# A two-layer transformer block in one launch: the keys of the second attention are split into two parts by GpSimd where they are made, and the first attention's lead-in and the middle stage's end are reordered

## The reference, cut to what matters

```
f1: 16 heads of 8, causal softmax(q k' / sqrt(8) - |i - j|) v, output projection
f2: each token goes to one of 8 experts (argmax): 128 -> 512 -> relu -> 128
f3: 16 heads of 64:
    q, k = rmsnorm(x Wq), rmsnorm(x Wk);  v = x Wv
    scores = q k' / 8 - (i - j) * slope_h * softplus(k . u_h / 8),  causal softmax, times v, projection
f4: 128 -> 512 gated, two 512 x 512 layers with gelu, -> 128
```

## Time and profile before

| | us |
|---|---|
| median of 3 runs | 2282.85 (2277.38 to 2283.62) |
| the profiled execution, its own time | 2285.02 |
| its span, first to last instruction | 2283.2 |
| PE busy | 2072.3 (91%) |
| DVE busy | 1513.8 (66%) |
| ACT busy | 1210.0 (53%) |
| POOL busy | 779.2 (34%) |

### The profile page before, as it was taken

The page is one execution under the profiler, slowest core; times in us unless marked ns, Lnnn a source line. Parts: engine busy times, 40 slices in busy tenths (PEclk is TensorE's granted clock), DMA queues, the critical chain, the costliest instruction groups (busy, mean ns, idle before and its releaser), DMA issues.

```text
span 2283.2 us, 34398 instructions
## 1 busy us (share of the span) xinstructions
PE 2072.3 (91%) x11728; PEld 1169.3 (51%) x11728; DVE 1513.8 (66%) x3409; ACT 1210.0 (53%) x1923; POOL 779.2 (34%) x480
## 2 busy tenths in 40 slices
PE   5899999998487999877999999999999999999998
PEld 2333333334476555544555555555555555655644
DVE  3877777774732778865888878888887875333311
ACT  2366666667343678853656555555565553223232
POOL 5000000000601111003777777777777773000000
PEclk7899999999588999986999999999999999999999
DMA  5233333111265579656666666666666667543300
GB/s 177 95 125 128 120 120 127 57 51 62 98 186 145 172 231 293 200 169 141 170 166 170 165 152 152 150 159 169 163 169 152 164 158 209 135 103 84 88 5 9
DMA packets 230189, 319.11 MB, mean 140 GB/s; under 512 B 22316, under 2 KB 152668, under 8 KB 229608
## 3 DMA queue, kind: packets, MB, share of 16 engines
q1 hardware_dynamic: 214712, 289.04, 46.2%
q0 software_dynamic: 7664, 24.39, 3.0%
q10 hardware_dynamic: 7640, 3.48, 0.5%
HBM read 176.91 MB, written 105.84 MB: 124 GB/s over the span
## 4 chain that ended last, share of the span: by engine, by line
PE 28%; DVE 16%; issue 8%; SPq 1%; DMA 1%; ACT 0%; DVEq 0%
PE ps L1252 10%; DVE a1mx L968 4%; PE ps L916 4%; DVE a1KB L982 3%; DVE a1mx L972 3%; PE ps L900 3%; DVE a1QB L982 3%; PE ps L870 2%; PE ps L901 2%; PE ps L1203 2%; DVE a1mx L965 2%; PE ps L1263 1%; PE ps L1240 1%; PE ps L1241 1%; DVE ps L965 1%
## 5 line engine op out<-in xcount | busy, mean ns | idle before, releaser
L1088 POOL TENSOR_TENSOR a1sum<-a1sum,a1prob 128x1024 f32<-128x1024 f32 (+3 forms) x256 | 489.0, 1910 | 64.9 <-ACT a1prob L1025 33.5
L1025 ACT ACTIVATE a1prob<-ps 128x512 f32<-128x512 f32 (+2 forms) x640 | 326.0, 562 | 252.7 <-PE ps L903 238.4
L468 DVE TENSOR_REDUCE a0grid<-ps 128x8 f32<-128x1024 f32 x288 | 346.7, 1221 | 118.9 <-PE ps L344 64.9
L569 ACT ACTIVATE a0prob<-ps 128x1024 f32<-128x1024 f32 x288 | 292.9, 1025 | 170.2 <-PE ps L370 91.3
L965 DVE CUSTOM_DVE_ANT_0 ps<-ps,c_mask_ij 128x128 f32<-128x128 f32 x496 | 262.7, 551 | 97.2 <-issue 95.5
L900 PE MATMUL ps<-a1QA,a1KA 69*128 69x512 f32 (+3 forms) x768 | 285.7, 379 | 5.8 <-PEq L33 3.4
L916 PE MATMUL ps<-a1prob,a1V 128*64 128x512 f32 (+3 forms) x1536 | 277.9, 505 | 0.0
L870 PE MATMUL ps<-a1KA,a1QA 68*128 68x128 f32 x744 | 241.7, 391 | 28.7 <-DVE a1mx L968 16.4
L901 PE MATMUL ps<-a1QB,a1KB 128*128 128x512 f32 (+3 forms) x768 | 264.4, 352 | 0.0
L916 PEld LDWEIGHTS ps<-a1prob,a1V 128*64 128x64 f32 x1536 | 104.4, 140 | 171.1 <-issue 144.2
L1085 POOL TENSOR_TENSOR a1sum<-a1prob 128x768 f32<-128x768 f32 x64 | 156.8, 2450 | 82.0 <-ACT a1prob L1025 79.9
(11 more groups left out here) (268 smaller groups left out, 3227.5 us busy)
## 6 DMA issues: line engine op xcount, KB each, us to landing
a1FK<-s_k SPq DMA_DIRECT2D x128, 256.0 KB, 5.3
a1FQ<-s_q SPq DMA_DIRECT2D x128, 256.0 KB, 5.8
s_xs<-c_zero POOLq DMA_DIRECT2D x19, 1024.0 KB, 9.0
s_q<-mqkT SPq DMA_DIRECT2D x32, 512.0 KB, 3.0
s_k<-mqkT SPq DMA_DIRECT2D x32, 512.0 KB, 3.0
s_v<-mv SPq DMA_DIRECT2D x32, 512.0 KB, 3.9
a1V<-s_v SPq DMA_DIRECT2D x32, 512.0 KB, 4.4
a1KA<-a1KB SPq DMA_DIRECT2D x64, 256.0 KB
```

The costliest lines, as they stand in the source:

```text
L468: dve.tensor_reduce(grid[g % 2][:, :, a:b + 1:b - a], banks(("max", k)), axis=AX.X, op=ALU.max).then_inc(s1_free, 1)
L569: act.activation(prob[:, :, a:b + 1:b - a, :], banks(("exp", q)), ACT.Exp).then_inc(p_full, 1)
L1025: act.activation(weights_of(g, u)[:, group[0]:group[-1] + 1, off:BANK], both(e, u, group), ACT.Exp).then_inc(weighed, 1)
L1088: pool.tensor_tensor(t[:, :, off:BANK], t[:, :, off:BANK], weights_of(g, u)[:, :, off:BANK], ALU.add).then_inc(summed, 1)
```

## The change

Four things are changed, and buffers are moved to make room for them.

1. **Keys split where they are made.** In the middle, POOL reads each turned tile of k (`qkT`), copies it to a rounded high part KH and subtracts to a low part KL (128 x 1024 each). SP stores both parts, so `k1` in DRAM has two planes; a tile's pair of stores is issued one tile later. The second attention loads high and low straight into KA and KB, so ACT's `split`, DVE's `lower` and the copies of keys go, in the loop and for pair 0 in the middle. For q all is as before, two calls of each in place of four.
2. **The places of what is left.** DVE's two `lower` calls stand at units 0 and 4, ahead of the jobs there; ACT's `split` at units 0 and 3, and the loads in SP's order around them. The q of pair 1 is rounded at the end of the middle.
3. **The first attention's lead-in.** EARLY is 13, there are three high and low buffers, the wait for stored chunks is taken out of `part`, ACT issues the load of BK after product 7 and not 15, and SP issues K and BQ of group 0 after the stores of chunk 2.
4. **The middle's end.** Half of the 24 maxima blocks stand before the last gates and half behind them.

```diff
-    EARLY, NPROD, COL = 17, len(products), dim + 1
+    PARTS3, EARLY, NPROD, COL = 3, 13, len(products), dim + 1
...
-        high, low = ([over(f"{n}{r}", [P, 2, CHUNK], F32R) for r in range(2)] for n in ("high", "low"))
+        high, low = ([over(f"{n}{r}", [P, 2, CHUNK], F32R) for r in range(PARTS3)] for n in ("high", "low"))
...
+            batch_stored(sp, 0)
             still(sp, Q[0], "q0", 0, loaded1[0])
-            sp.wait_ge(cleared, 1)
-            load_second(sp, 0)
             for c in range(2, chunks):
                 store(c)
-                if c == 3:
+                if c == 2:
+                    sp.wait_ge(cleared, 1)
+                    load_second(sp, 0)
+                if c == 4:
                     sp.wait_ge(cleared, 2)
                     load_first(sp, 1)
...
-            for n in range(6, EARLY - 1):
+            for n in range(6, 8):
                 drain(n)
             act.wait_ge(cleared_first, 1)
+            batch_stored(act, 0)
             moving(act, BK[0], "k0", 0, loaded1[0])
-            for n in range(EARLY - 1, NPROD):
+            for n in range(8, NPROD):
                 drain(n)
...
+        def load_a(x, h):
+            if x >= NB:
+                nc.sync.wait_ge(valued, unit(x - NB, NU - 1) + 1)
+            nc.sync.dma_start(KA[x % NB][0:dim, h, :].bitcast(F32), heads_of(x, scr["k1"][0])[:, h, :]).then_inc(loaded_e[x % NB], 16)
+        def load_b(x, k):
+            h, r = divmod(k, 2)
+            if x >= NB:
+                nc.sync.wait_ge(valued, unit(x - NB, NU - 1) + 1)
+            nc.sync.dma_start(KB[x % NB][r * dim:(r + 1) * dim, h, :].bitcast(F32), heads_of(x, scr["k1"][r])[:, h, :]).then_inc(loaded_k[x % NB], 16)
...
-        SPLIT, LOW, PARTS, N_E = 4, 4, 8, 5
+        SPLIT, LOW, PARTS, N_E, N_K = 2, 2, 4, 5, 4
...
         def sync_program():
+            for h in range(2):
+                copy_high(1, h)
+                load_a(1, h)
             load_e(1)
-            for k in range(SPLIT):
-                copy_high(1, k)
             for k in range(PARTS):
                 load_f(2, k)
+            for h in range(2):
+                load_a(2, h)
             load_e(2)
+            for k in range(N_K):
+                load_b(2, k)
...
+            def lower(x, h):
+                dve.wait_ge(rounded, SPLIT * x + h + 1)
+                low = QB[x % NB][0:dim, h, :]
+                dve.tensor_tensor(low, FQ[x % 2][0:dim, h, :], low.bitcast(F32), ALU.subtract).then_inc(lowered, 1)
             for g in range(G):
                 for u in range(NU):
-                    if g == 0 and 2 <= u < 6:
-                        lower(1, u - 2)
-                    at_units = (2, 6, 10, 11) if g > 0 else (6, 7, 10, 11)
-                    if g + 2 < G and u in at_units:
-                        lower(g + 2, at_units.index(u))
+                    if g == 0 and u < 2:
+                        lower(1, u)
+                    if u == 0 and 0 < g < G - 1:
+                        lower(g + 1, 1)
+                    if u == TILES and g + 2 < G:
+                        lower(g + 2, 0)
...
-                    at_units = (0, 3, 4, 5) if g > 0 else (4, 5, 6, 7)
-                    if g + 2 < G and u in at_units:
-                        split(g + 2, at_units.index(u))
+                    if g + 2 < G and u in (0, 3):
+                        split(g + 2, (0, 3).index(u))
...
-            if n == LAST:
-                here += [("max", k, 0) for k in range(NM)] + [("turn", 0, 0)]
+            here += [("max", k, 0) for k in range(NM // 2)] if n == LAST else []
             here += [("aug", c, 0) for c in turn_gates.get(n, ())]
+            here += [("max", k, 0) for k in range(NM // 2, NM)] + [("turn", 0, 0)] if n == LAST else []
...
+        def store_k(tile):
+            sp = nc.sync
+            sp.wait_ge(k_low, tile + 1)
+            for r, part in enumerate((pair0.KH, pair0.KL)):
+                sp.dma_start(scr["k1"][r, :, tile * P:(tile + 1) * P].rearrange("(k p) i -> p k i", p=P), part[tile % 2][:, :, :].bitcast(F32)).then_inc(k_out[tile % 2], 16)
...
+            def part(tile):
+                high, low, source = pair0.KH[tile % 2][:, :, :], pair0.KL[tile % 2][:, :, :], qkT[tile % 2][:, WK, :, :]
+                pool.wait_ge(weighted, 4 * tile + 4)
+                if tile > 1:
+                    pool.wait_ge(k_out[tile % 2], 32 * (tile // 2))
+                pool.tensor_copy(high, source).then_inc(k_high, 1)
+                pool.wait_ge(k_high, tile + 1)
+                pool.tensor_tensor(low, source, high.bitcast(F32), ALU.subtract).then_inc(k_low, 1)
+            gather(0)
+            gather(1)
...
+            for tile in range(NTILE):
+                if tile % TILES == 0 and tile // TILES + 2 < steps:
+                    gather(tile // TILES + 2)
+                part(tile)
...
+            act.wait_ge(pair0.loaded_f[1], 16 * 4)
+            for head in range(2):
+                act.activation(pair0.QB1[:, head, :], pair0.FQ[1][:, head, :], ACT.Copy).then_inc(pair0.rounded, 1)
```

196 lines of the change are left out of this document (103 added, 93 removed).

## The result

The changed kernel takes 2268.25 us in the median of 8 runs (2266.37 to 2274.33), the kernel before 2280.98 beside it: a ratio of 0.9945, 95% interval 0.9933 to 0.9957. It is faster by half a per cent, 13 us where I said 28. The profiled execution has a span of 2268.6 us against 2283.2.

What follows compares the result with a forecast made beforehand. PE was taken as nearly full, 94% in the tiles and 97% in the loop with DVE at 86%. The terms -10 + 23 - 1 - 12 - 28 = -28 gave 2255 us from a median of 2282.85, range 2222 to 2281.

Steps and rivals of the forecast that it cites:

- Lead-in, -10: First attention's start: earlier BK load -7, second PE stall gone -5.4, more products among the maxima +2.4; -6 to -14 us.
- The steady first attention is not touched, so this is kept: First attention: the lead-in's gain of 10 us was to last to the stage's end.
- GpSimd in the middle, +23: Tiles of q, k, v: GpSimd's subtraction blocks DVE's small z, delaying PE: 21 us, plus 2 for joins; bounds 0 and 75.
- (c): Rival, tiles: nearly every tile is hit, 31 x 2.2 = 68 us against 51 saved elsewhere, 2300 us; chance 0.09.
- Hits can thus not follow each other: about 10 instead of 16: Tiles: after a hit the next z comes 0.4 us earlier and waits only for GpSimd's copy; 21 us in all.
- So I cost it at nothing: Middle's DMA: the extra plane's 10 us of landing time is covered by two tiles of buffers; 0, up to 5 us.
- The middle's end, -1: End of the middle: the start hangs on pair 0's row landing in place of the gates'; -1 us (0 to -2).
- Start of the loop, -12: Loop's first group: first job of pair 1 5.8 us earlier, key subtractions left out up to 6 more; -5 to -15 us.
- The loop, -28: Second attention's loop: fewer PE waits for DVE, 1.0 us a group over 28 groups; -28 us (-14 to -36).
- (a): Rival, tiles: GpSimd's subtraction never gets ahead of DVE's z; 0 to 2 in place of 23, 2233 us; chance 0.28.
- (b): Rival, loop: DVE was the true bound; -70 in place of -28, 2213 us; chance 0.09.
- (d): Rival, loop: it gives nothing since PE is at 97%, 2283 us; chance 0.09 together with lead-in and start giving half.

Runs made afterwards that it cites:

- e9: The kernel before with the lead-in's part of the change alone: 2280.4 us, ratio 0.9998 to the kernel before.
- e5: Changed kernel with GpSimd's copy and subtraction held back until DVE's next z, and at chunk ends its join and normalisation, are done: 2247.5 us, ratio 0.9866.
- e13: e5 with the low plane of the keys made but neither stored nor loaded, the high plane loaded instead: 2239.9 us, ratio 0.9828.
- e12: Changed kernel with DVE's two query subtractions back at their old units 6 and 11 of a group: 2421.2 us, ratio 1.0631.
- e11: Kernel before without DVE's two key subtractions a group in the loop, all else in place: 2264.6 us, ratio 0.9937.
- e10: Changed kernel with all maxima of pair 0 ahead of the last gates, as in the kernel before: 2273.3 us, ratio 0.9974.
- e16: Changed kernel with GpSimd held back, first pairs' loads in every second item, group 0's row first in SP's order, and pair 1's slopes first: 2234.2 us, ratio 0.9809.
- e8: Changed kernel with ACT's rounding of pair 2 in the loop's first group at units 4 and 5, DVE's subtraction at 6: 2268.4 us, ratio 0.9940.
- run 0: Not an experiment: a stretch of each group of the loop, where one of seven jobs waited 0.54 us for DVE; forecast gain 0.6 us a group.
- run 1: Not an experiment: a stretch of each group of the loop; first scores to denominators took 6.02 us before, 5.47 after the change.
- run 2: Not an experiment: a stretch of each group of the loop, with its subtractions behind the jobs that PE waits for; forecast gain nothing.
- e14: Kernel before with DVE's two query subtractions moved from units 6 and 11 to 4 and the next group's 0, nothing removed: 2295.0 us, ratio 1.0050.
- e7: Changed kernel with SP issuing group 0's row first, then Q and BK of group 2, then K and BQ of group 1: 2263.4 us, ratio 0.9935.

## Why the prediction was right in its direction and wrong in its size

**Lead-in, -10: wrong, it gave 3 us in one trace and nothing in the median (e9).** The term of 7 for BK gave 4.5: its load is used 9.3 us behind the end of ACT's last issue, and I had allowed some 7. The other stall went, the four products cost some 0.7 instead of 2.4, and the row's maxima came 9.2 us earlier, so up to there the sum was right. What failed is the step "The steady first attention is not touched, so this is kept". I followed the loads as far as the first maxima and not to the first scores. The row that the scores wait for is issued on the same queue, and I did not ask what stands ahead of it at its new time.

**GpSimd in the middle, +23: mis-sized, 36.3.** The mechanism and its place were as forecast: z, a good third of the tiles, 2.3 us each, and PE's product behind. The margin was not, and that it came out is luck. GpSimd needs 0.08 to 0.09 us from its copy to its subtraction, where I took 0.14. The late tiles come 0.08 us too late and not 0.02, and the others get through by 0.01 us or less, where I had 0.06: a little less, and nearly every tile would have been hit, my rival (c). Two steps failed. "Hits can thus not follow each other: about 10 instead of 16" is half wrong: 13 tiles are hit (counted from 0: 5 and 6, and 19 to 22, in a row). Behind 8 of the 13 the next z falls into the copy as I said, behind 4 it is hit again. 13 x 2.13 is 28 us, PE's waits ahead of the k products grew by 21.8, and e5 puts all that goes with hits at 21, so this term alone was right within 2 us. The larger failure is "So I cost it at nothing", for DMA: it costs 12.8 us (e13). The sum beside it had the right size, about 10 us of landing time, and I trusted two tiles of buffers to hide it. But a buffer's slack helps only until the queue is behind by more, and here it stays behind for every store as long as the pairs are loaded: DMA is at 1.07 of its share with or without the extra plane. The bounds of 0 to 5 for it were too narrow.

The Trainium skill, page "SBUF — State Buffer", section "Who interferes with whom", has the rule of the exclusive lock for whoever comes first. It holds in both directions here: in e12 DVE waits 1.9 us for GpSimd, in e11 GpSimd 0.8 us for DVE.

**The middle's end, -1: right,** with -0.8, and the start hangs on the row's landing as I said. That e10 is 0.3% slower without it was not in my sum: I had not seen that SP's order puts the last stores of k behind the gates'.

**Start of the loop, -12: mis-sized, -4.4.** The copies went out at once, at 1064.28 us, but the first job did not come 5.2 us behind the first scores, but 9.2, since it waits for five DMAs, of which two are now loads of keys from DRAM and the fifth the slopes (L806). With the slopes first it still waits for the keys (e16). The step "the same 3.4 us behind a last issue" took the landing of a copy within SBUF for that of every load. "That is hidden by the jobs, or it costs half the gain" was decided by e8 for the first. What I left out altogether is that PE runs at half clock in much of this group, before and after the change, so "DVE sets the pace of this group" is not true for most of it, and the 6 us for DVE's three subtractions had no place. The -4.4 is itself what this execution gave: four runs with the same code took 2 us more than the kernel before, with the clock back 38 us behind the first scores and not 21. What makes the clock come back early or late stays open.

**The loop, -28: right in kind, low by a third; it gave 41.5.** Run 0 gave 0.70 (forecast 0.6), run 1 0.55 (0.4), run 2 nothing, as I said. The 0.15 a run that I took off for the new places never came, and the period fell by 1.24 us over 28 periods, 35 us. Some 8 us more are not the period: five groups of the kernel before took 27.2 to 29.0 us in that execution, with the clock at 0.79 in the window of the first. After the change no steady group does. That these followed PE's small waits for DVE, which are gone, is likely by e12 and e14 but not shown. For run 1 I had read group 30 rightly (no `lower` at all, 5.47 us) and credited the wrong `lower` with it.

**The rivals.** (a) did not happen on the chip by itself, and e5 makes it: with the hits gone the kernel is at 2247, not at 2233, since DMA is left. (b) is out: with DVE out of the way the loop is bound by PE at 99.6% and 25.3 us a group, not by 24. (c) and (d) did not occur. The two large errors of the sum have opposite signs and cancel by luck: the middle cost 13 us more than I said, and the loop gave 13 more. What is left of the miss are the 7 us each of lead-in and start. Both are the same mistake, a start that was followed to the next wait and no further.

## What to carry to other kernels

A DMA that gets ready earlier may land hardly earlier when it is issued on a queue that has much ahead of it at its new time: for each step moved forward, list what is ahead of it in its queue then, and put the few bytes on which everybody waits first (the row of maxima here, 5.5 us).

A DVE instruction with two SBUF operands beside a long GpSimd instruction was free here or waited for all that was left of it, and 0.1 us decided. Such a pair should be put in order by a semaphore, not left to chance: holding GpSimd back gave 21 us here, and e12 shows what chance can do, 150 us for two instructions moved.

When an engine's utilisation is near full in a stage, do the sum of bytes as well as that of instructions. And an idle gap in front of a TensorE that is otherwise full is priced by its length only if the clock stays up.

## What was not expected of the hardware

A stop of PE of 1.2 us (the one shown of e14) or 2.0 us (e12), in a stretch that is full on both sides, was followed by 4 to 10 us at about 0.50 of the clock, which cost some 3.3 us more than the stop itself. Stops of 0.2 to 0.8 us were mostly not (31 in the kernel before, with five longer groups).

After a stage's start at half clock the time until the clock came back differed between executions of nearly the same code, 21 to 25 us or 36 to 38, which makes a step of some 5 us in the length of a group that no wait explains.

Of two DMAs of 8 KB each, issued behind 16 loads of a few partitions each, the second took 8 us to land (L227 in the changed kernel), with the DMA share at 0.31 from 78 to 88 us. With these loads behind it (e7) it took 1.9. The share over all engines does not say that a queue is free.
